# Two gated attention and expert layers on one core: the second normalisation moved to the next slot, and the work between the score products dealt out anew

## The chip, the cores and the metric

One core of one Trainium2 chip. The time is that of one execution on the device, in microseconds (us). Before the change three runs took 878.42, 873.18 and 877.70 us, median 877.7. The engines are TensorE (PE in the rows, its weight loads PEld), VectorE (DVE), ScalarE (ACT), GpSimd (POOL) and SyncE (SP), which issues most transfers.

## What is computed

32 sequences of 128 tokens, 128 wide, go through two layers. Cut to its core the reference is

```python
x = x + tanh(g_xattn[0]) * attention0(layernorm(x), ctx)   # 16 heads of 8, biases, output product Wo
x = x + tanh(g_ffn[0]) * experts0(layernorm(x))            # 8 experts, capacity routing, hidden 256
x = x + tanh(g_xattn[1]) * attention1(layernorm(x), ctx)   # 16 heads, no biases, no output product
x = x + tanh(g_ffn[1]) * experts1(layernorm(x))            # best 2 of 8 experts, hidden 512
```

The attentions are softmax(q k scale) v over 128 keys. The router of each expert layer is a product of the normalised tokens with a 128x8 matrix.

## The kernel before

Each layer has two stages: an attention stage over 16 pairs of sequences, and an expert stage over tiles of 256 tokens. The change touches only the attention stages.

**Slots.** An attention stage is a software pipeline. `pair_slots` walks 23 slots, p from -4 to 18, and in each slot every engine's `slot` function works on up to eight pairs, each at another step: n (four ahead) has its first normalisation's statistics taken, f (three ahead) is transposed and gets queries and keys, r (two ahead) its values' projection, m (one ahead) its score maxima, a (this one) the scores of its first sequence, b (one behind) those of its second sequence and the weighted values of both, z (two behind) its output and new x, and y (three behind) the router's product. A slot in which all are present is called full here: p from 3 to 11, and 12 but for n. The order on each engine is written out by hand and is a fixed queue; engines meet at semaphores (`wait_ge`).

**Units.** A slot has eight units. On TensorE unit i is `scores_for_maxima(i)` (L577: four products whose bank VectorE reduces, `maxima(i)`, L789), then a score product `scores` (L565: units 0 to 3 are the second sequence of b, numbers 4 to 7; units 4 to 7 the first of a), whose bank ScalarE turns into PT by an exponential (L443). There are two banks for each (MB, ST), so product i waits until number i-2 has been read. Between the units stand the fillers.

**Fillers of TensorE before.** Unit 0: the transpose of a's maxima MX, `values(b, 0)` (V0, L683, 16 products), the two transposes of OK (z, layer 0). Unit 1: the two transposes of XN (f). Unit 2: the output product (L613, z, layer 0, reads OKT) and the router's product (L619, y, reads NT, into bank PA). Unit 3: key and query products (L630, L632, f). Unit 4: V1. Unit 5: value projection (L647, r). Unit 6: four transposes of OT (b). Unit 7: the two transposes of N (z).

**ScalarE** copies between its exponentials: NT, OKT, XT (L461), LG (router's result, L466), HL (high halves of queries and keys, L474), OT (L484), VA (values, L490) and writes N, the second normalisation (L496, two instructions). **VectorE** between its maxima: MH (shifted maxima, L798), statistics of n (L774 to L806), the new x of z (L814), the statistics of z with MINUS and VE_N (L826, L827), the low halves of HL (L834), XN (L845) and the division by the sums of b (L854, L855, into OK). **GpSimd** raises the variances to the power -0.5 (L387, L391) and multiplies by minus the mean (L392); in layer 0 it adds the output bias to x (L398). **SyncE** sends MH into the row that the scores read (L298), loads the spread queries and keys (L306, L307) and writes HL out (L317). In layer 1 it also loads expert weights (L292) in eight slots.

PF is one bank for three uses: XN's transposes and the value projection in its first half, N's transposes in its second. Waits on `v_kept`, `front_kept` and `n_kept` keep its users apart.

## Time and profile before

| | us |
|---|---|
| median of three runs | 877.7 |
| lowest, highest | 873.18, 878.42 |
| the profiled execution's own time | 874.29 |
| its span in the profile | 872.5 |
| TensorE busy (matmul rows) | 536.8 (62%) |
| VectorE busy | 484.0 (55%) |
| ScalarE busy | 349.5 (40%) |
| GpSimd busy | 285.4 (33%) |

The span is 1.8 us shorter than the execution's time. The attention stages run from about 16 to 227 us and from about 400 to 595 us; in the expert stages and in the routing between them the change edits nothing. Busy shares over the whole span are means over stages that have different limits, so the rows further below are taken inside the attention stages.

### The profile page before, as it was taken

The page shows a single profiled execution, that of the slowest core. Times are in us where ns is not written, and L with a number is a line of the kernel's source. Part 1 is how long each engine was busy: PE and PEld are TensorE (multiplying, and loading weights), DVE is VectorE, ACT ScalarE, POOL GpSimd, SP SyncE. Part 2 cuts the span into 40 slices and gives each one's busy share as a digit, 9 for nine tenths or more (in the row PEclk, how much of TensorE's full clock was granted, in tenths as well). Part 3 has the DMA queues.
Part 4 walks back from the last instruction along what each step waited for, and adds up shares of the span by engine and source line. Part 5 has one row for each costly group of instructions (what it writes and reads, how often), then busy time and mean ns, then how long its engine had stood idle before and what let it go on. Part 6 is the DMA issues. An engine that isn't in the chain of part 4 may idle for free.

```text
span 872.5 us, 16776 instructions
## 1 busy us (share of the span) xinstructions
PE 536.8 (62%) x5459; PEld 427.9 (49%) x5459; DVE 484.0 (55%) x1521; ACT 349.5 (40%) x795; POOL 285.4 (33%) x342
## 2 busy tenths in 40 slices
PE   1688999987200008862798999861000199999960
PEld 0566666664100007651566667640000199999960
DVE  4668888874588203434789999847200034444324
ACT  1157777766100004321266777762000055555530
POOL 6102222201001754771011111010777435555550
PEclk9979999999555559995699999995555599999995
DMA  7543333320000312325455553200311212222219
GB/s 251 151 136 88 87 88 88 88 58 2 0 0 3 101 55 81 106 77 137 124 144 148 158 153 97 59 2 2 101 53 52 62 53 73 75 71 75 74 37 288
DMA packets 94628, 76.37 MB, mean 88 GB/s; under 512 B 13904, under 2 KB 88528, under 8 KB 94096
## 3 DMA queue, kind: packets, MB, share of 16 engines
q1 hardware_dynamic: 86432, 57.05, 24.0%
q0 software_dynamic: 7040, 14.53, 4.9%
q10 hardware_dynamic: 1072, 3.73, 1.3%
q8 instruction: 46, 0.75, 0.4%
q14 instruction: 38, 0.31, 0.1%
HBM read 45.54 MB, written 33.46 MB: 91 GB/s over the span
## 4 chain that ended last, share of the span: by engine, by line
PE 41%; POOL 15%; DVE 12%; issue 10%; DMA 9%; ACT 7%; SPq 4%; ACTq 1%; DVEq 0%; POOLq 0%
POOL dispatched L407 10%; PE bank L730 8%; PE bank L740 8%; PE bank L683 6%; PE bank L577 4%; PE bank L551 4%; POOL returned L414 4%; PE bank L565 4%; DMA QS_N<-MH 3%; DVE PT L979 2%; DVE MX L789 2%; ACT N L496 2%; DMA returned<-PT,META_ROW 2%; ACT PT L443 2%; PE bank L630 1%
## 5 line engine op out<-in xcount | busy, mean ns | idle before, releaser
L789 DVE TENSOR_REDUCE MX<-bank 128x4 f32<-128x512 f32 x256 | 172.9, 685 | 45.0 <-PE bank L577 44.8
L443 ACT ACTIVATE PT<-bank 128x512 f32<-128x512 f32 x256 | 152.7, 600 | 107.2 <-PE bank L565 106.4
L414 POOL DMA_INDIRECT returned<-PT,META_ROW x124 | 119.1, 961 | 111.8 <-DVE PT L1070 87.1
L521 ACT ACTIVATE XGT<-bank 128x256 f32<-128x256 f32 x62 | 23.8, 384 | 260.3 <-PE bank L551 260.3
L551 PE MATMUL bank<-CONST,PT 128*128 128x128 f32 x124 | 25.9, 292 | 148.2 <-issue 142.1
L577 PE MATMUL bank<-KS,QS_N 96*128 96x128 f16 x1024 | 104.8, 229 | 12.1 <-DMA KS<-spread 10.0
L565 PE MATMUL bank<-QS_N,KS 98*128 98x512 f16 x256 | 99.2, 391 | 8.2 <-DMA QS_N<-MH 7.8
L740 PEld LDWEIGHTS bank<-WALL,HT 128*128 128x128 f32 x808 | 98.8, 192 | 10.2 <-issue 7.0
L740 PE MATMUL bank<-WALL,HT 128*128 x808 | 101.1, 276 | 3.9 <-issue 1.5
L730 PE MATMUL bank<-XGT,XT_HL_WR 128*128 128x256 f32 x404 | 100.7, 389 | 0.0
L577 PEld LDWEIGHTS bank<-KS,QS_N 96*128 96x128 f16 x1024 | 78.5, 104 | 34.1 <-DMA KS<-spread 11.6
L1058 DVE COPY META_ROW<-PT 128x2 int32<-128x2 int32 x62 | 11.3, 182 | 150.8 <-DMA PT<-dispatched 111.4
L407 POOL DMA_INDIRECT dispatched<-N,SLOT x64 | 62.2, 971 | 96.7 <-DVE EX L1041 77.8
L551 PEld LDWEIGHTS bank<-CONST,PT 128*128 128x128 f32 x124 | 15.5, 149 | 152.9 <-issue 143.4
L730 PEld LDWEIGHTS bank<-XGT,XT_HL_WR 128*128 128x128 f32 x404 | 74.1, 196 | 7.9
L387 POOL TENSOR_TENSOR RSTD<-VE,EXPO 128x2 f32<-128x2 f32 x32 | 22.3, 698 | 156.0 <-DVE VE L806 155.9
L532 ACT ACTIVATE HT<-bank,XT_HL_WR 128x256 f32<-128x256 f32 x156 | 64.0, 472 | 21.4 <-PE bank L730 21.4
L683 PE MATMUL bank<-PT,VA 128*32 128x128 f32 x2048 | 69.6, 277 | 2.7 <-ACT LG L466 2.7
L391 POOL TENSOR_TENSOR RSTD_N<-VE_N,EXPO 128x2 f32<-128x2 f32 x32 | 22.1, 691 | 144.6 <-DVE VE_N L827 144.6
L683 PEld LDWEIGHTS bank<-PT,VA 128*32 128x32 f32 x2048 | 52.4, 110 | 20.3 <-issue 14.7
L1066 DVE TENSOR_TENSOR PT<-bank,WALL 128x256 f32<-128x256 f32 x39 | 16.6, 424 | 57.5 <-PE bank L740 52.5
L1053 DVE COPY XT_HL_WR<-WALL 128x516 f32 (+1 forms) x62 | 23.9, 385 | 31.2 <-issue 19.2
(172 smaller groups left out, 830.5 us busy)
## 6 DMA issues: line engine op xcount, KB each, us to landing
spread<-XT_HL_WR SPq DMA_DIRECT2D x128, 64.0 KB, 2.1
PT<-dispatched SPq DMA_DIRECT2D x62, 130.0 KB, 2.1
QS_N<-spread SPq DMA_DIRECT2D x128, 48.0 KB
KS<-spread SPq DMA_DIRECT2D x32, 192.0 KB
WALL<-in_w SPq DMA_DIRECT2D x8, 578.0 KB, 4.0
CT<-in_ctx SPq DMA_DIRECT2D x32, 128.0 KB, 2.7
spread<-XT_HL_WR SPq DMA_DIRECT2D x32, 128.0 KB, 2.3
dispatched<-in_pads SPq DMA_DIRECT2D x2, 1040.0 KB, 5.7
```

Source lines behind the costliest of these rows:

```text
L407: pool.indirect_dma_start(xs[layer][:, :], bass.IndirectOffsetOnAxis(ap=SLOT[:, k, b:b + 1], axis=0), (N, N2)[k][:, b, :], None).then_inc( ...
L414: pool.indirect_dma_start(ys[layer][:, :], bass.IndirectOffsetOnAxis(ap=META_ROW[:, a.f, c:c + 1], axis=0), YS[:, a.f, c, :], None).then_i ...
L443: nc.scalar.activation(PT[:, c, 4 * g:4 * g + 4, :].rearrange("p j q -> p (j q)"), ST[i % 2][:, :], ACT.Exp, scale=SCALE[layer]).then_inc( ...
L532: last = nc.scalar.activation(HT[:, a.u, m, :], bank[2 * a.u + m // 2][:, TILE * (m % 2):TILE * (m % 2) + TILE], ACT.Gelu, bias=WR[:, a.t, ...
L551: return nc.tensor.transpose(to, of, ident[0:n, 0:n])
L565: nc.tensor.matmul(ST[i % 2][:, :].rearrange("p (j q) -> p j q", j=J), KS[0:98, x.r, g, c * P:(c + 1) * P], QS[0:98, x.r, J * g:J * g + J, ...
L577: last = nc.tensor.matmul(MB[i % 2][:, j * P:(j + 1) * P], QS[0:96, m.r, J * g + j, c * P:(c + 1) * P], KS[0:96, m.r, g, c * P:(c + 1) * P ...
L683: last = nc.tensor.matmul(PA[32 * g:32 * g + 32, 256 * c + P * (j // 2):256 * c + P * (j // 2) + P], VA[:, b.r, c, head(g, j), :], PT[:, c ...
L730: last = nc.tensor.matmul(bank[2 * a.u + m // 2][:, TILE * (m % 2):TILE * (m % 2) + TILE], WR[:, a.t, m * P:(m + 1) * P], XGT[:, a.u, :], ...
L740: last = nc.tensor.matmul(bank[6 + a.u][:, c * D:(c + 1) * D], HT[:, a.u, m, c * P:(c + 1) * P], WALL[:, bass.ds(r + (W1COLS[layer] + m * ...
L789: V.tensor_reduce(out=MX[:, m.u, 2 * J * g + c:2 * J * (g + 1):2], in_=MB[i % 2][:, :].rearrange("p (j k) -> p j k", j=J), op=ALU.max, axi ...
L1053: V.tensor_copy(WR[:, a.t, 0:W1COLS[layer]], WALL[:, bass.ds(r, W1COLS[layer])]).then_inc(w_kept, 1)
```

## The change

It moves work between units and slots, and three small operations between engines:

- The second normalisation (N), its transposes and the router's product are now done in one slot, by pair y: N is written on ScalarE in unit 2, transposed in unit 4 ahead of that unit's score product, copied to NT after unit 5's exponential, and multiplied in unit 6. Before, N and its transposes came at the end of z's slot and the product in the next slot. The router's product now goes to bank PF instead of PA, and V1 has no wait for `lg_kept` any more.
- The division by the sums (reciprocal and OK) is done in slot z behind maxima 2, no longer in slot b behind maxima 7. OK's transposes are in unit 3, the output product in unit 5, the new x behind maxima 6, and its statistics behind maxima 7.
- TensorE's other fillers: XN's transposes to unit 0, V0 to unit 1, the value projection to unit 2, V1 to unit 5, OT's transposes to unit 7. Key and query products stay in unit 3. XN is made behind maxima 3, not 6.
- VE (one a slot), MINUS and VE_N (one each) are computed on GpSimd instead of VectorE. GpSimd's order within the slot becomes n, bias, z.

```diff
@@ GpSimd
                         pool.wait_ge(x_norm, before(n.g - 1))
+                        chain.link(nc.gpsimd.tensor_scalar(out=VE[:, n.u, :], in0=MV[:, n.u, :, 1], scalar1=LN_EPS, scalar2=None, op0=ALU.add))
                         nc.gpsimd.tensor_tensor(out=RSTD[:, n.u, :], in0=VE[:, n.u, :], in1=EXPO[:, :], op=ALU.pow).then_inc(x_rstd, 1)
...
+                    if z:
+                        pool.wait_ge(n_stats, z.g + 1)
+                        pool.wait_ge(n_copied, before(z.g - 1))
+                        nc.gpsimd.tensor_scalar(out=MINUS[:, z.u, :], in0=MV_N[:, z.u, :, 0], scalar1=-1.0, scalar2=None, op0=ALU.mult)
+                        chain.link(nc.gpsimd.tensor_scalar(out=VE_N[:, z.u, :], in0=MV_N[:, z.u, :, 1], scalar1=LN_EPS, scalar2=None, op0=ALU.add))
+                        chain.link(nc.gpsimd.tensor_tensor(out=RSTD_N[:, z.u, :], in0=VE_N[:, z.u, :], in1=EXPO[:, :], op=ALU.pow))
@@ ScalarE
+                    exponentials(b, 6)
+                    if y:
+                        act.wait_ge(n_rstd, y.g + 1)
+                        for c in range(2):
+                            last = nc.scalar.activation(N[:, y.b + c, 0:D], batch(y, c), ACT.Identity,
+                                                        scale=RSTD_N[:, y.u, c:c + 1], bias=OFFSET_N[:, y.u, c:c + 1])
+                        last.then_inc(n_copied, 1)
+
                     exponentials(b, 7)
...
@@ TensorE
                     scores_for_maxima(4)
+                    if y:
+                        pe.wait_ge(n_copied, y.g + 1)
+                        if r:
+                            pe.wait_ge(v_kept, r.g + 1)
+                        pe.wait_ge(lg_kept, y.g)
+                        for c in range(2):
+                            last = transpose(PF[:, 256 + c * P:256 + (c + 1) * P], N[:, y.b + c, 0:D])
+                        last.then_inc(n_t, 1)
                     scores(a, 0)
-                    if b:
-                        if y:
-                            pe.wait_ge(lg_kept, y.g + 1)
-                        values(b, 1)
...
+                    if y:
+                        pe.wait_ge(n_kept, y.g + 1)
+                        for c in range(2):
+                            last = nc.tensor.matmul(PF[:, 256 + E * c:256 + E * c + E], NT[:, c * P:(c + 1) * P],
+                                                    WG[:, layer, :], start=True, stop=True)
+                        last.then_inc(lg_done, 1)
@@ VectorE
-                        link(stats(n, STATS, MV[:, n.u]))
-                        V.tensor_scalar(out=VE[:, n.u, :], in0=MV[:, n.u, :, 1], scalar1=LN_EPS, scalar2=None,
-                                        op0=ALU.add).then_inc(x_stats, 1)
+                        stats(n, STATS, MV[:, n.u]).then_inc(x_stats, 1)
                     maxima(2)
+                    if z:
+                        dve.wait_ge(o_t, z.g + 1)
+                        dve.wait_ge(x_new, z.g)
+                        if layer == 0:
+                            dve.wait_ge(ok_t, z.g)
...
+                        stats(z, STATS_N, MV_N[:, z.u]).then_inc(n_stats, 1)
```

The removals mirror these additions. SyncE's queue is the same row for row. In the rows below "bank<-CONST,N" is a transpose of N, and the same for OK, OT, MX and XN; after the change the score products are L567, the products for maxima L579, transposes L553, and ScalarE's exponentials L446.

TensorE in layer 0, a full slot before, from the value projection of unit 5 to the end of unit 7:

```order
L647 MATMUL bank<-WSQ,CT 128x128 [waits v_kept,front_kept]
L647 MATMUL bank<-WSQ,CT 128x128
L577 MATMUL bank<-KS,QS_N 128x128 [waits m_read]
L577 MATMUL bank<-KS,QS_N 128x128 x3
L565 MATMUL bank<-QS_N,KS 128x512 [waits exp_done]
L551 MATMUL bank<-CONST,OT 128x128 [waits x_new,av_kept]
L551 MATMUL bank<-CONST,OT 128x128 x3
L577 MATMUL bank<-KS,QS_N 128x128 [waits m_read]
L577 MATMUL bank<-KS,QS_N 128x128 x3
L565 MATMUL bank<-QS_N,KS 128x512 [waits exp_done]
L551 MATMUL bank<-CONST,N 128x128 [waits front_kept,n_kept,v_kept,n_copied]
L551 MATMUL bank<-CONST,N 128x128
```

Each of the last two fillers follows, by one unit, the product that its copy waits for. The same engine after the change, from unit 3 to unit 4's scores:

```order
L579 MATMUL bank<-KS,QS_N 128x128 [waits m_read]
L579 MATMUL bank<-KS,QS_N 128x128 x3
L567 MATMUL bank<-QS_N,KS 128x512 [waits exp_done]
L624 MATMUL bank<-CT,WSQ 128x256 [waits m_split,hl_done,cx1]
L626 MATMUL bank<-XT_HL_WR,WSQ 128x256 [waits front_kept]
L553 MATMUL bank<-CONST,OK 128x128 [waits o_kept]
L553 MATMUL bank<-CONST,OK 128x128
L579 MATMUL bank<-KS,QS_N 128x128 [waits m_read]
L579 MATMUL bank<-KS,QS_N 128x128 x3
L553 MATMUL bank<-CONST,N 128x128 [waits lg_kept,v_kept,n_copied]
L553 MATMUL bank<-CONST,N 128x128
L567 MATMUL bank<-QS_N,KS 128x512 [waits exp_done,shift0]
```

N's transposes now stand ahead of a score product, and OK's ahead of unit 4. The rest of that slot, from unit 5 into unit 7:

```order
L579 MATMUL bank<-KS,QS_N 128x128 [waits m_read]
L579 MATMUL bank<-KS,QS_N 128x128 x3
L567 MATMUL bank<-QS_N,KS 128x512 [waits exp_done]
L683 MATMUL bank<-PT,VA 32x128 [waits exp_done]
L683 MATMUL bank<-PT,VA 32x128 x15
L651 MATMUL bank<-WSQ,OKT 128x128 [waits ok_kept]
L651 MATMUL bank<-WSQ,OKT 128x128
L579 MATMUL bank<-KS,QS_N 128x128 [waits m_read]
L579 MATMUL bank<-KS,QS_N 128x128 x3
L567 MATMUL bank<-QS_N,KS 128x512 [waits exp_done]
L660 MATMUL bank<-WG,NT 128x8 [waits n_kept]
L660 MATMUL bank<-WG,NT 128x8
```

The output product and the router's product, which stood next to each other, are now a unit apart, each behind another filler.

ScalarE in layer 0, before, from unit 3's exponential to N:

```order
L443 ACTIVATE PT<-bank 128x512 [waits s_banks]
L466 ACTIVATE LG<-bank 128x16 [waits lg_done]
L443 ACTIVATE PT<-bank 128x512 [waits av_done,s_banks]
L474 ACTIVATE XT_HL_WR<-bank,VEC 128x256 [waits written0,qk_done]
L474 ACTIVATE XT_HL_WR<-bank,VEC 128x256
L443 ACTIVATE PT<-bank 128x512 [waits s_banks]
L484 ACTIVATE OT<-bank 128x512 [waits o_t,av_done]
L443 ACTIVATE PT<-bank 128x512 [waits s_banks]
L490 ACTIVATE VA<-bank 128x16x2x8 [waits av_done,v_done]
L496 ACTIVATE N<-X,OFFSET_N,RSTD_N 128x128 [waits n_rstd]
L496 ACTIVATE N<-X,OFFSET_N,RSTD_N 128x128
```

And after, from unit 2's exponential:

```order
L446 ACTIVATE PT<-bank 128x512 [waits s_banks]
L460 ACTIVATE N<-X,OFFSET_N,RSTD_N 128x128 [waits n_rstd]
L460 ACTIVATE N<-X,OFFSET_N,RSTD_N 128x128
L446 ACTIVATE PT<-bank 128x512 [waits s_banks]
L468 ACTIVATE VA<-bank 128x16x2x8 [waits av_done,v_done]
L446 ACTIVATE PT<-bank 128x512 [waits av_done,s_banks]
L477 ACTIVATE XT_HL_WR<-bank,VEC 128x256 [waits written0,qk_done]
L477 ACTIVATE XT_HL_WR<-bank,VEC 128x256
L485 ACTIVATE OKT<-bank 128x256 [waits wo_done,ok_t]
L446 ACTIVATE PT<-bank 128x512 [waits s_banks]
```

N, which stood near the end of the slot behind the values' copy, now stands ahead of it and of unit 3's exponential; OKT has moved behind HL, and NT behind unit 5's exponential.

## Rows read from the trace of the kernel before

**Rows 1.** Busy time by stretch: full slots of layer 0, then of layer 1.

```profile
100.00:120.00 20.00, 17.99 (x250) 13.41 (x249) 17.80 (x55) 14.34 (x35) 3.94 (x7) 1.00 0.32 88
520.00:540.00 20.00, 18.58 (x263) 14.29 (x260) 19.13 (x61) 14.60 (x34) 3.16 (x6) 1.00 0.37 102
```

**Rows 2.** Timeline of ScalarE (start us, us): copies of OT, one a slot.

```profile
70.18 0.59 ACT L484 ACTIVATE OT<-bank 128x512 f32<-128x512 f32 x1
...
178.72 0.59 ACT L484 ACTIVATE OT<-bank 128x512 f32<-128x512 f32 x1
...
208.72 0.59 ACT L484 ACTIVATE OT<-bank 128x512 f32<-128x512 f32 x1
...
451.35 0.59 ACT L484 ACTIVATE OT<-bank 128x512 f32<-128x512 f32 x1
...
501.80 0.59 ACT L484 ACTIVATE OT<-bank 128x512 f32<-128x512 f32 x1
...
549.90 0.59 ACT L484 ACTIVATE OT<-bank 128x512 f32<-128x512 f32 x1
...
576.97 0.59 ACT L484 ACTIVATE OT<-bank 128x512 f32<-128x512 f32 x1
```

**Rows 3.** Waits, 70 to 178 us, then 446 to 550 (us, times, longest).

```profile
PEld bank L551 <- ACT N L496: 7.6, 10, 0.8
PEld bank L613 <- ACT OKT L456: 6.3, 10, 0.6
...
PEld bank L551 <- ACT OT L484: 6.2, 10, 0.6
...
PEld bank L565 <- DMA QS_N<-MH: 3.4, 5, 1.1
```

**Rows 4.** Timeline of TensorE in a full slot of layer 0.

```profile
104.91 0.44 PE L551 MATMUL bank<-CONST,N 128*128 128x128 f32 x2 [0.42 <-ACT N L496]
...
105.18 0.39 PE L577 MATMUL bank<-KS,QS_N 96*128 96x128 f16 x4
...
105.41 0.38 PE L565 MATMUL bank<-QS_N,KS 98*128 98x512 f16 x1
...
105.83 1.08 PE L683 MATMUL bank<-PT,VA 128*32 128x128 f32 x32
...
106.84 0.44 PE L551 MATMUL bank<-CONST,OK 128*128 128x128 f32 x2
...
108.68 0.71 PE L613 MATMUL bank<-WSQ,OKT 128*128 128x128 f32 x4 [0.30 <-ACT OKT L456]
...
109.23 0.51 PE L619 MATMUL bank<-WG,NT 128*128 128x8 f32 x4
...
109.60 0.38 PE L577 MATMUL bank<-KS,QS_N 96*128 96x128 f16 x4
...
110.90 0.39 PE L577 MATMUL bank<-KS,QS_N 96*128 96x128 f16 x4
```

**Rows 5.** Timeline of ScalarE in the same slot.

```profile
101.19 0.83 ACT L474 ACTIVATE XT_HL_WR<-bank,VEC 128x256 f16<-128x256 f32 x2
...
103.70 0.40 ACT L490 ACTIVATE VA<-bank 128x256 f32<-128x256 f32 x1
...
103.96 0.89 ACT L496 ACTIVATE N<-X,OFFSET_N,RSTD_N 128x128 f32<-128x128 f32 x2
...
105.83 0.60 ACT L443 ACTIVATE PT<-bank 128x512 f32<-128x512 f32 x1 [0.48 <-PE bank L565]
```

**Rows 6.** Groups by shape, GpSimd and VectorE (busy us, mean ns).

```profile
L391 POOL TENSOR_TENSOR RSTD_N<-VE_N,EXPO 128x2 f32<-128x2 f32 x32 | 22.1, 691 | 144.6 <-DVE VE_N L827 144.6
...
L377 POOL MEMSET QS_N<- 96x2048 f32 x4 | 7.3, 1825 | 0.2
...
L392 POOL TENSOR_TENSOR OFFSET_N<-MINUS,RSTD_N 128x2 f32<-128x2 f32 x32 | 6.3, 196 | 2.5
...
L806 DVE TENSOR_SCALAR VE<-MV 128x2 f32<-128x2 f32 x32 | 5.4, 169 | 1.1
```

More of the change, by code:

```diff
@@ L635, in slot @@
                     scores(a, 0)
[L636 to L639 removed]
                     scores_for_maxima(5)
                     scores(a, 1)
[L643 to L645 removed]
+                    if b:
+                        values(b, 1)
+                    if z and layer == 0:
+                        pe.wait_ge(ok_kept, z.g + 1)
@@ L653, in slot @@
+                    scores(a, 3)
                     if b:
@@ new lines, in slot @@
+                    maxima(3)
+                    if n:
+                        dve.wait_ge(x_rstd, n.g + 1)
+                        dve.wait_ge(front_t, before(n.g - 1))
+                        for c in range(2):
+                            last = V.tensor_scalar(out=XN[:, n.u, c * D:(c + 1) * D], in0=batch(n, c), scalar1=MV[:, n.u, c, 0:1],
+                                                   scalar2=RSTD[:, n.u, c:c + 1], op0=ALU.subtract, op1=ALU.mult)
+                        last.then_inc(x_norm, 1)
```

161 lines of the change are left out of this document (59 added, 102 removed).

## Prediction

> **What bounds the kernel now.** I began with the busy time by stretch [rows 1]. In full slots of the first attention stage TensorE's matmul rows are busy 18.0 of 20 us and VectorE 17.8, ScalarE 14.3; in the second stage it is 18.6, 19.1 and 14.6. The granted clock there is 1.00 of full speed, 2.4 GHz, so the clock is not what costs time here. Two engines stand near nine tenths, and neither is full: what is left is waits inside the slot.
>
> Second, the length of a slot, taken as the distance between two copies of OT (one a slot) [rows 2]. Layer 0: 70.18 to 178.72 is ten slots of 10.85 us; the three that follow, in which the fronts run out, take 30.0 together. Layer 1: 451.35 to 501.80 is five slots of 10.09, in which the expert weights are loaded beside the work; 501.80 to 549.90 five of 9.62; the next three take 27.1.
>
> Third, who TensorE waits for [rows 3]: three copies by ScalarE, once a slot each, 0.76, 0.63 and 0.62 us in the weight-load rows of ten slots: for N, for OKT (layer 0 alone) and for OT. Each copy is asked for one unit after the product that it copies, which is too soon. In time of the slot they are shorter, since part of it lies beside the product before. The timeline of a slot [rows 4] gives the price of the steps, from start to start: four products for the maxima 0.23, a score product and MX's transpose together 0.42 (I split it 0.22 and 0.20), a half of the values 1.01, N's pair of transposes 0.27, the output product 0.55, the router's 0.37. From 109.60 to 110.90 there is a unit's maxima and scores, 0.45, and so 0.85 for the key and query products. From these rows I estimate the rest: the value projection at half of the last, 0.43, the pairs for OK and XN like N's, OT's four transposes twice that, 0.54. Eight units of 0.445 and these (two halves of the values) sum to 9.37; the waits are 10.85 - 9.37 = 1.48, some 0.5 each.
>
> **The change, by the same rows.** TensorE loses and gains no instruction; V0 now follows a score product, as V1 did, which costs 0.09 more, so 9.46 without waits. What changes is how far each product stands behind its copy. I lay the new slot out from its first maxima product at 0. A score product is followed by its exponential 0.42 later (105.41, 105.83), ScalarE starts its next instruction 0.12 to 0.14 before the last one's end (103.70 + 0.40, 103.96), and TensorE goes on 0.05 after a copy's end [rows 4, 5].
> - N's transposes (unit 4). Unit 2's scores start at 2.69, the exponential at 3.11, the two N copies at 3.59 (0.89 for both), unit 3's exponential at 4.36, V's copy at 4.84, ending 5.24. TensorE, past the value projection (2.91), unit 3 (3.34), keys and queries (3.78), OK's transposes (4.63) and unit 4's maxima (4.90), comes to them at 5.13 and starts at 5.29: wait 0.16.
> - The output product (end of unit 5). Scores of unit 4 at 5.56, exponential 5.98, the two halves of HL at 6.46 (0.83), OKT at 7.17 (0.38, like V's copy), end 7.55. TensorE, after unit 5 and V1, is there at 7.32 and starts at 7.60: wait 0.28.
> - The router's product (unit 6) comes at 8.59, with NT's copy done at 8.29: no wait. Before, it stood right behind the output product and hid in its wait.
> - OT's transposes (unit 7). Unit 6's scores at 8.37, exponential 8.79, OT's copy 9.27 to 9.86. TensorE is there at 9.41: wait 0.50, as now.
> New layer 0 slot: 9.46 + 0.16 + 0.28 + 0.50 = 10.40, 0.45 less than 10.85. Ten slots give 4.5.
>
> VectorE: the three small operations on the variance and mean leave it, about 0.17 us each [rows 6], with two waits for its own results; it keeps 17.8/20 of 10.85 = 9.65 less about 0.4, so 9.2 in a slot: below 10.40. The division by the sums (reciprocal and OK) now stands behind maxima 2, done at about 4.3 (maxima 2 from 2.84, 0.6, two operations with 0.8), and its transposes are asked for at 4.6; X's update ends at about 9.65, before OT's transposes at 9.91. Both are covered, by some 0.3 us. If VectorE ran later than this, TensorE would wait for it here.
>
> Layer 1 has no OKT and no output product: 9.46 - 0.27 - 0.55 = 8.64, but with less in front of them N's pair waits 0.43, the router's product 0.07 and OT's 0.43: 9.57 against 9.62. The same sum for the kernel before (9.37 - 0.82 and two waits of 0.5) gives 9.55 where 9.62 was measured, so 0.07 is missing in it; five slots give between 0.25 and -0.1, and I take 0. In the slots beside the weight load, unit 4's scores wait for the two small transfers from MH (five times, up to 1.1 us [rows 3]). Between MX's transpose and that score TensorE does more than before: the value projection and N's pair with its wait, 1.1 us, come in, and the router's 0.37 goes behind. With 0.7 more cover most of the wait goes, and those slots come to the others' length: 5 x (10.09 - 9.62) = 2.4. If nothing of it goes, 0.
>
> SyncE's own order is the same. The spread reads are issued after MH's in both, and the sum above keeps hi and low parts of HL at 7.3 and 8.2 of the slot; I count nothing, and bound it at 0 to 0.3 us per layer 1 slot, should they land too late for a shorter slot.
>
> GpSimd: per slot it gets three operations of 128x2 more. The nearest row is the small product at 196 ns; the far one the fill of 96x2048 at 1825 ns [rows 6]. I take 0.2 each. VectorE's second statistics end 0.55 into the next slot; two such operations, the power of 0.69, the product of 0.20 and the gaps give the scale at 2.2, and ScalarE wants it at 3.59. So the cost is nothing, hidden beneath units 0 to 2, as long as one operation is under about 0.9. For the first normalisation the cover ends at 0.94.
>
> Fill and drain. Ahead of the ten slots of each layer stands one more that is nearly full; the two give 0.4 and 0.3. The drain slots, laid out in the same way, come to 9.9 + 9.4 + 8.3 = 27.6 for 30.0 and 25.8 for 27.1. That is 3.7 at most; these have less to hide behind, so the other end is 0, and I take 2.4. After the last pair the work is a chain with nothing beside it: GpSimd's operations on it cost two times 0.2 to 0.3 per layer, and N's pair stands ahead of the last output product: a loss of 0.5 per layer, 1.0 together. The first slots wait for transfers and XN; I count nothing, between -1 and +1.
>
> **Sum.** 4.5 + 0 + 2.4 + 0.7 + 2.4 - 1.0 = 9.0, against the profiled execution's 874.29: **865.3 us**. That execution is near the fast end of the runs shown, 3.4 under their median of 877.7; I keep its time as the base. About 1% (8.7 us) is what a measurement of this kernel can tell from no change.
>
> **Where the skill speaks against it.** The moved operations leave VectorE, but they run on GpSimd while VectorE works. In the rows of before the power on GpSimd has a mean of 691 ns beside a VectorE that is nine tenths busy [rows 1, 6]; whether VectorE is held while it runs, the rows do not tell. The Trainium skill (SBUF — State Buffer, Who interferes with whom) says that a VectorE instruction in a two-port mode, which `tensor_scalar` can be, and a GpSimd instruction shut each other out for their whole length, while VectorE's `tensor_reduce` never contends. By that rule the new operations are harmless where they fall beside maxima, which is where I expect all three; no run here shows them in their new places.
>
> **Rivals.**
> *The gain stays in layer 0 (870).* VectorE has 0.9 of 20 us idle in layer 1 [rows 1], 0.4 per slot. If the new operations on GpSimd hold VectorE back, 3 x 0.2 = 0.6 per slot, or if HL's second part now waits on ScalarE's first, layer 1 is bound as before; the drain gives nothing. What is left is 4.5 + 0.4 - 1.0 = 3.9, or 870.4; with 0.2 lost in each of ten slots of layer 1, 872. For it: VectorE's 19.1 of 20. Against: three operations leave it. That the change only moves its waits about, as my 0.50 for OT says of one of them, would end at 870 to 874 too. The skill's rule above is one way into this rival.
> *Slower, by GpSimd's chain (879).* N's copy now stands ahead of unit 3's exponential, V's copy and the first scores, so if the scale is late, everything is. It decides from 0.9 us per small operation. At 1.2 each the scale comes 0.6 late: 24 slots give 14 us, and with this in place of nothing 865.3 + 14 = 879; at the far row's 1.8, 1.9 late, 46 us, 910. For it: nothing stands between, and two engines feed it. Against: 196 ns in the nearest row.
> *More than forecast (859).* The waits of the three copies gone altogether in layer 0's ten slots would be 9.4 more; half of that, with all of the drain's 3.7, gives 859.
>
> **How the numbers follow.** The forecast with what lies around it, 861 to 869: 0.50. More: 0.10. Gain in layer 0 alone or moved waits: 0.29. Slower: 0.11. Faster by over 1% (under 865.6 by the execution's own time, under 869 by the median) takes all of the second, 0.40 of the first and 0.06 of the third: 0.56. Slower by over 1%: 0.10, the slower rival but for its mildest prices; within 1%: the rest, 0.34. The range 856 to 874 leaves out the slow rival and the ends of the others.
>
> **What would show it.** In the profile after: slots of the first layer at about 10.4; TensorE's wait for OKT halved, that for N near 0.3 in the weight-load rows, that for OT unchanged; no wait for POOL before N; layer 1 slots all near 9.6; VectorE's rows at L789 with more idle time ahead of them in layer 0. I am wrong if the slots stay above 10.6, if a wait for VectorE (OK, X, maxima) appears on TensorE, or if N waits for GpSimd.

## Result: 1.3% faster, and the profile after

The changed kernel took 863.02, 864.47, 866.71 and 866.29 us, median 865.38; the kernel before, with one more run on the same chip, has a median of 876.28. The ratio is 0.9869, with a 95% interval of 0.9841 to 0.9896 (the two medians alone differ by 10.9 us, or 1.2%). Two executions of the experiments below are not in their ratios, a slow one of e12 (910.81 us at a granted clock of 0.741, where the others have 0.825 to 0.830) and one of e9 that took 2696.48 us. The profiled execution took 863.02 us, its span is 861.2 where it was 872.5: 11.3 us less.

Busy time by stretch, in the columns of [rows 1]:

```profile
100.00:120.00 20.00, 18.91 (x261) 14.89 (x260) 17.82 (x50) 14.54 (x36) 6.02 (x14) 1.00 0.35 95
505.00:525.00 20.00, 19.11 (x284) 14.28 (x277) 18.96 (x51) 15.02 (x34) 5.19 (x14) 1.00 0.47 129
```

In the first layer TensorE went from 18.0 to 18.9 of 20 us busy, and VectorE stayed at 17.8: the same work in less time would have raised it to 18.7, but the three small operations are gone from it. In the second layer the row of 20 us shows 19.0 for VectorE, nearly as before, but that stretch is not a whole number of slots. Over five whole slots VectorE is busy 44.2 of 47.6 us (492.88 to 540.47), where it was 45.8 of 48.1 (501.80 to 549.90): it has a little more idle time there too.

Copies of OT on ScalarE, one a slot, as [rows 2]. The copy stands a unit later in its slot now, so only distances may be compared with before:

```profile
70.31 0.59 ACT L497 ACTIVATE OT<-bank 128x512 f32<-128x512 f32 x1
...
132.31 0.59 ACT L497 ACTIVATE OT<-bank 128x512 f32<-128x512 f32 x1
...
143.20 0.59 ACT L497 ACTIVATE OT<-bank 128x512 f32<-128x512 f32 x1
...
174.45 0.59 ACT L497 ACTIVATE OT<-bank 128x512 f32<-128x512 f32 x1
...
201.52 0.59 ACT L497 ACTIVATE OT<-bank 128x512 f32<-128x512 f32 x1
...
444.40 0.59 ACT L497 ACTIVATE OT<-bank 128x512 f32<-128x512 f32 x1
...
492.88 0.59 ACT L497 ACTIVATE OT<-bank 128x512 f32<-128x512 f32 x1
...
540.47 0.59 ACT L497 ACTIVATE OT<-bank 128x512 f32<-128x512 f32 x1
...
565.72 0.59 ACT L497 ACTIVATE OT<-bank 128x512 f32<-128x512 f32 x1
```

From 70.31 to 174.45 are ten slots, 104.1 us where there were 108.5. They are not alike: 70.31 to 132.31 is six of 10.33 each, and the one that follows takes 10.89. The three drain slots take 27.07 for 30.0. In layer 1 the five slots beside the weight loads take 48.5 for 50.5, the next five, called plain here, 47.6 for 48.1 (9.52 each), the three of the drain 25.25 for 27.1. (The eight loads are issued in slots 2 to 9, so the plain five have the last two of them beside them, in both kernels, and are hardly longer for it.)

Waits of TensorE's weight loads in layer 0, 70 to 170 us, to be held against [rows 3]:

```profile
PEld bank L553 <- ACT OT L497: 7.4, 10, 1.1
...
PEld bank L651 <- ACT OKT L485: 4.6, 9, 0.5
...
PEld bank L553 <- issue: 1.8, 9, 0.2
PEld bank L567 <- DMA QS_N<-MH: 0.8, 2, 0.6
```

The wait for N's two instructions is not in the list any more. What N's transposes still wait for stands under "issue", 0.2 in nine slots, and is read below. The wait for OKT has gone from 0.63 to 0.51 each, that for OT is longer (0.74 against 0.62 each). A new row stands at the end: scores that wait for MH's transfer, 0.8 us in two places of layer 0, one of which is the long slot.

The same slot of layer 0 as in [rows 4, 5], by its landmarks. It starts with its first maxima product at 102.44:

```profile
102.44 0.39 PE L579 MATMUL bank<-KS,QS_N 96*128 96x128 f16 x4
...
104.42 0.20 POOL L401 TENSOR_TENSOR OFFSET_N<-MINUS,RSTD_N 128x2 f32<-128x2 f32 x1
...
105.91 0.87 ACT L460 ACTIVATE N<-X,OFFSET_N,RSTD_N 128x128 f32<-128x128 f32 x2
...
107.16 0.38 ACT L468 ACTIVATE VA<-bank 128x256 f32<-128x256 f32 x1
...
107.61 0.20 PEld L553 LDWEIGHTS bank<-CONST,N 128*128 128x128 f32 x2 [0.20 <-issue]
107.64 0.41 PE L553 MATMUL bank<-CONST,N 128*128 128x128 f32 x2
...
109.95 0.71 PE L651 MATMUL bank<-WSQ,OKT 128*128 128x128 f32 x4 [0.24 <-ACT OKT L485]
...
110.95 0.51 PE L660 MATMUL bank<-WG,NT 128*128 128x8 f32 x4
...
111.64 0.59 ACT L497 ACTIVATE OT<-bank 128x512 f32<-128x512 f32 x1
```

N's scale is ready at 104.62, N begins at 105.91, its transposes at 107.64, the output product at 109.95, the router's at 110.95, OT's copy at 111.64. Counted from 102.44 these are 2.18, 3.47, 5.20, 7.51, 8.51 and 9.20.

N's transposes follow the end of V's copy (107.16 + 0.38 = 107.54) by 0.07 us, while N itself was written by 106.78; V's copy is one of the three things that they wait for (`v_kept`). In layer 1 it is the same with a longer wait: V's copy ends at 518.21, the weight load for N starts at 518.28 after 0.42 idle. The profile names no releaser in either place, but the times leave V's copy.

The operations that GpSimd took over (mean ns behind the busy time), as [rows 6]:

```profile
L398 POOL TENSOR_SCALAR MINUS<-MV_N 128x2 f32<-128x2 f32 x32 | 7.5, 233 | 182.2 <-DVE MV_N L777 182.2
...
L387 POOL TENSOR_SCALAR VE<-MV 128x2 f32<-128x2 f32 x32 | 7.0, 219 | 96.5 <-DVE MV L777 96.5
```

**Where 11.3 us came from,** by the same landmarks in both traces: ten full slots of layer 0 4.4; ten of layer 1 2.5 (2.0 of it beside the weight loads); the slot ahead of each ten 1.05; three drain slots of each layer 2.9 and 1.8; all else inside the attention stages 0.1; and between and behind the attention stages, where nothing was changed, 1.45 was lost.

Of the 1.05, some 0.7 is no gain of the change. The slot ahead of layer 0's ten took 10.60 before and 9.87 after, but in e9 below, whose layer 0 is the kernel before's, it took 9.94. In the kernel before the granted clock stood at 0.50, which is 1.2 GHz, from 58.0 to 61.5 us, and so within that slot (59.58 to 70.18); in e9 it was back at 1.00 by 61.0, where the slot begins (61.07).

### The profile page after: what moved, and what is told of

Its sections match the earlier page's. It is cut to its first block, busy times and chain, and to the rows that moved or that the text cites. A ratio compares the mean times of both kernels' runs of the same rounds, so it can differ in the third digit from the quotient of the medians.

```text
span 861.2 us, 16742 instructions
## 1 busy us (share of the span) xinstructions
PE 532.4 (62%) x5459; PEld 427.2 (50%) x5459; DVE 476.6 (55%) x1425; ACT 350.0 (41%) x795; POOL 308.3 (36%) x438
## 4 chain that ended last, share of the span: by engine, by line
PE 43%; POOL 15%; issue 10%; DVE 10%; DMA 10%; ACT 6%; SPq 5%; ACTq 1%; DVEq 0%; POOLq 0%
POOL dispatched L410 11%; PE bank L730 8%; PE bank L740 8%; PE bank L553 6%; PE bank L683 5%; PE bank L579 5%; PE bank L567 5%; POOL returned L417 4%; DMA QS_N<-MH 3%; DMA returned<-PT,META_ROW 2%; DVE PT L975 2%; ACT OT L497 2%; SPq L317 2%; PE bank L624 1%; PE bank L651 1%
## 5 line engine op out<-in xcount | busy, mean ns | idle before, releaser
L446 ACT ACTIVATE PT<-bank 128x512 f32<-128x512 f32 x256 | 151.7, 597 | 91.3 <-PE bank L567 90.1
L553 PE MATMUL bank<-CONST,PT 128*128 128x128 f32 x124 | 26.1, 294 | 147.7 <-issue 142.1
L579 PE MATMUL bank<-KS,QS_N 96*128 96x128 f16 x1024 | 103.1, 225 | 16.8 <-DMA KS<-spread 12.3
L567 PE MATMUL bank<-QS_N,KS 98*128 98x512 f16 x256 | 97.8, 387 | 6.4 <-DMA QS_N<-MH 6.1
L579 PEld LDWEIGHTS bank<-KS,QS_N 96*128 96x128 f16 x1024 | 76.8, 102 | 41.1 <-DMA KS<-spread 16.6
L553 PEld LDWEIGHTS bank<-CONST,PT 128*128 128x128 f32 x124 | 15.5, 148 | 152.2 <-issue 143.4
L398 POOL TENSOR_SCALAR MINUS<-MV_N 128x2 f32<-128x2 f32 x32 | 7.5, 233 | 182.2 <-DVE MV_N L777 182.2
L387 POOL TENSOR_SCALAR VE<-MV 128x2 f32<-128x2 f32 x32 | 7.0, 219 | 96.5 <-DVE MV L777 96.5
```

Of the source, the lines that this page charges most:

```text
L446: nc.scalar.activation(PT[:, c, 4 * g:4 * g + 4, :].rearrange("p j q -> p (j q)"), ST[i % 2][:, :], ACT.Exp, scale=SCALE[layer]).then_inc( ...
L553: return nc.tensor.transpose(to, of, ident[0:n, 0:n])
L567: nc.tensor.matmul(ST[i % 2][:, :].rearrange("p (j q) -> p j q", j=J), KS[0:98, x.r, g, c * P:(c + 1) * P], QS[0:98, x.r, J * g:J * g + J, ...
L579: last = nc.tensor.matmul(MB[i % 2][:, j * P:(j + 1) * P], QS[0:96, m.r, J * g + j, c * P:(c + 1) * P], KS[0:96, m.r, g, c * P:(c + 1) * P ...
```

## Experiments

Slot lengths are those of the profiled execution; ratios are to the kernel before on the same chip.

**e1: N's move alone.** To the kernel before; N's old block on ScalarE and the router's old product into PA go as well, and LG's copy moves to the end of the slot and reads PF:

```diff
                     exponentials(b, 4)
-                    if y:
-                        act.wait_ge(n_t, y.g + 1)
-                        act.wait_ge(lg_done, y.g)
-                        nc.scalar.activation(NT[:, :], PF[:, 256:512], ACT.Copy).then_inc(n_kept, 1)
...
+                    if y:
+                        act.wait_ge(n_rstd, y.g + 1)
+                        for c in range(2):
+                            last = nc.scalar.activation(N[:, y.b + c, 0:D], batch(y, c), ACT.Identity,
+                                                        scale=RSTD_N[:, y.u, c:c + 1], bias=OFFSET_N[:, y.u, c:c + 1])
+                        last.then_inc(n_copied, 1)
                     exponentials(b, 7)
...
                     exponentials(a, 0)
+                    if y:
+                        act.wait_ge(n_t, y.g + 1)
+                        act.wait_ge(lg_done, y.g)
+                        nc.scalar.activation(NT[:, :], PF[:, 256:512], ACT.Copy).then_inc(n_kept, 1)
...
                     scores_for_maxima(4)
+                    if y:
+                        pe.wait_ge(n_copied, y.g + 1)
...
+                            last = transpose(PF[:, 256 + c * P:256 + (c + 1) * P], N[:, y.b + c, 0:D])
+                        last.then_inc(n_t, 1)
                     scores(a, 0)
...
                     scores(a, 3)
-                    if z:
-                        pe.wait_ge(n_copied, z.g + 1)
+                    if y:
+                        pe.wait_ge(n_kept, y.g + 1)
...
-                            last = transpose(PF[:, 256 + c * P:256 + (c + 1) * P], N[:, z.b + c, 0:D])
-                        last.then_inc(n_t, 1)
+                            last = nc.tensor.matmul(PF[:, 256 + E * c:256 + E * c + E], NT[:, c * P:(c + 1) * P],
+                                                    WG[:, layer, :], start=True, stop=True)
+                        last.then_inc(lg_done, 1)
```

> The kernel before, with one part of the change alone: N, its transposes, NT and the router's product in y's slot (N behind the exponential of unit 2, transposes ahead of unit 4's scores, product at the slot's end into PF); every other filler stays. Theory (each wait of TensorE for a copy costs its length once a slot and is independent of the others): the wait for N, 0.5 to 0.6 us of the slot, goes, those for OKT and OT stay; layer 0 slots 10.85 to 10.3 or 10.4, layer 1 plain slots 9.62 to 9.1 or 9.2, in all 10 to 13 us faster than before, so as much as the whole change. Rival (the waits are one budget, and what one gives back the next takes, or VectorE does): slots fall by under 0.2 in layer 0 and not at all in layer 1, in all under 4 us.

Measured: 870.84 us, ratio 0.9949 (0.9921 to 0.9977), 5 us faster. In layer 0 the theory holds to the tenth: ten slots of 10.37, so one wait removed gives its 0.48, and the waits for OKT and OT stay as they were (0.63 and 0.62 each). That is practically all that the whole change gives in a full slot there, 0.52. In layer 1 the plain slots are 9.35 to 9.5, shorter than the changed kernel's own 9.5 (in e1 V's copy is not ahead of N's transposes, which start with no wait), but the slots beside the weight loads are 9.5 to 13.5. The total was forecast at twice what came or more. Its cause is in one row of the waits, 440 to 530 us, and in this piece of the timeline of its worst slot:

```profile
PE bank L564 <- DMA QS_N<-MH: 7.5, 6, 2.5
```

```profile
456.98 0.58 SPq L292 DMA_DIRECT2D WALL<-in_w  x1
457.76 1.20 SPq L298 DMA_DIRECT2D QS_N<-MH  x2
...
463.16 0.61 PE L564 MATMUL bank<-QS_N,KS 98*128 98x512 f16 x1 [2.49 <-DMA QS_N<-MH]
```

MH is sent out 0.8 us behind a weight load of 578 KB, and its scores begin 5.4 us later, 2.5 of it idle. The slot is 4.1 longer than a plain one, so the wait is not all of it: the granted clock was 1.00 until TensorE had stood idle in that wait, and 0.50 from about 462.5 to 469.5. (This execution, the profiled one, took 875.44 us, 4.6 over e1's median, so its stalls are above the usual.) The same place in the changed kernel:

```profile
494.72 0.59 SPq L292 DMA_DIRECT2D WALL<-in_w  x1
495.72 1.18 SPq L298 DMA_DIRECT2D QS_N<-MH  x2
```

```profile
499.45 0.38 PE L567 MATMUL bank<-QS_N,KS 98*128 98x512 f16 x1
```

There 3.7 us lie between issue and use and nothing waits. Without a stall it is 2.75 us in e1, 2.7 to 3.0 in the kernel before's plain slots, 3.7 in the changed one. So the moves of the other fillers, which give nothing in layer 0's full slots, are what covers this transfer in layer 1. e1 has less cover on one more ground: MH is sent 1.75 us behind its transpose, not 1.27, because VectorE still divides by the sums just before it takes up MH.

**e2: the three small operations back on VectorE,** in the changed kernel.

```diff
-                        nc.gpsimd.tensor_scalar(out=MINUS[:, z.u, :], in0=MV_N[:, z.u, :, 0], scalar1=-1.0, scalar2=None, op0=ALU.mult)
-                        chain.link(nc.gpsimd.tensor_scalar(out=VE_N[:, z.u, :], in0=MV_N[:, z.u, :, 1], scalar1=LN_EPS, scalar2=None, op0=ALU.add))
...
-                        stats(z, STATS_N, MV_N[:, z.u]).then_inc(n_stats, 1)
+                        link(stats(z, STATS_N, MV_N[:, z.u]))
+                        V.tensor_scalar(out=MINUS[:, z.u, :], in0=MV_N[:, z.u, :, 0], scalar1=-1.0, scalar2=None, op0=ALU.mult)
+                        V.tensor_scalar(out=VE_N[:, z.u, :], in0=MV_N[:, z.u, :, 1], scalar1=LN_EPS, scalar2=None,
+                                        op0=ALU.add).then_inc(n_stats, 1)
```

VE goes back in the same way.

> The changed kernel with its three small operations (VE, MINUS, VE_N) back on VectorE. Theory (VectorE is not what bounds the changed kernel): slots stay at 10.33 in layer 0, within 0.05, and at 9.5 in layer 1, within 0.1; the whole within 1.5 us of the changed kernel, that is 864 to 867. Rival (VectorE had become the bound and the move to GpSimd is where the gain is from): layer 1 slots back to 9.7 or more, the whole 3 to 8 us slower than the changed kernel, 868 to 873.

Measured: 862.31 us, ratio 0.9859 (0.9815 to 0.9904), within the interval of the changed kernel. Seven of its ten full slots of layer 0 are 10.33, three are 10.6 to 11.0, which are waits for MH. Of layer 1's plain slots two are 9.5, and three are 9.8 to 10.1 with waits for MH of 0.2 to 0.4 us: with the small operations back, VectorE sends MH 1.47 us behind its transpose, not 1.27. So one sign of the rival, slots of 9.7 or more, was there in part, but by a transfer and not by VectorE's share, and the total does not show it. The move to GpSimd is worth nothing in the total that can be measured. VectorE does not bound the changed kernel.

**e3: OT's copy before unit 6's exponential, not after it; e4: and X's update before maxima 6.** Both on the changed kernel:

```diff
-                    exponentials(a, 2)
                     if b:
                         act.wait_ge(av_done, 2 * b.g + 2)
                         act.wait_ge(o_t, b.g)
                         nc.scalar.activation(OT[:, :], PA[:, :], ACT.Copy).then_inc(av_kept, 1)
 
+                    exponentials(a, 2)
                     exponentials(a, 3)
```

And in e4 alone:

```diff
-                    maxima(6)
                     if z:
                         if layer == 0:
...
                                                    in1=two(z).rearrange("p c d -> p (c d)"), op0=ALU.mult, op1=ALU.add).then_inc(x_new, 1)
+                    maxima(6)
                     maxima(7)
```

> The changed kernel with OT's copy on ScalarE ahead of unit 6's exponential, not behind it. Theory (TensorE's last wait in each slot is for this copy alone, 0.37 us in time of the slot): in layer 1, where the new x waits for nothing of TensorE, slots go from 9.50 to 9.1 or 9.2; in layer 0 X's update, which ends 0.3 us before the transposes start, is next, and the slot goes from 10.33 to 10.1 or 10.25 with a wait for X on TensorE; in all 5 to 9 us faster than the changed kernel, 857 to 860. Rival (VectorE or the MH transfers bound the slot by now): no slot shorter by over 0.1, within 2 us of the changed kernel.

> As e3, and X's update on VectorE ahead of maxima 6 instead of behind it, so that it is done 0.6 us sooner. Theory: layer 0 slots at 9.95 to 10.05, no wait for X left; layer 1 as in e3; in all 2 to 4 us faster than e3. Rival (maxima 6, now later, holds the next maxima products; or MH's transfers are late): layer 0 no faster than e3.

Measured: e3 858.85 us, ratio 0.9827 (0.9786 to 0.9869). Layer 0 slots are 10.17, plain slots of layer 1 down to 9.15. TensorE's own rows in layer 0 name who is late next:

```profile
PE bank L553 <- DVE X L841: 2.8, 10, 0.6
PE bank L651 <- ACT OKT L485: 2.1, 9, 0.2
```

The transposes of OT now wait for X, 0.28 a slot, in the place that the theory gave. e4: 854.49, ratio 0.9775 (0.9731 to 0.9819), layer 0 slots 9.79. e4 is 4.4 us faster than e3, where 2 to 4 were expected, and no wait for X is left; its slot of layer 0 is shorter than the 9.95 that was expected. I had taken the wait from TensorE's rows, 0.37, which leave out what lies beside the product before. From start to start it is 0.53: in the changed kernel unit 7's score product starts at 111.53, takes 0.22 until the next can start, and OT's transposes start at 112.28. e4's slot is 0.54 shorter than 10.33. The plain theory, that each wait of TensorE for a copy is worth its length until the next in line is reached, is shown by both, with the length taken from start to start.

**e5 and e6: weight loads in slots 11 to 18** instead of 2 to 9, on e1 and on e4.

```diff
-                if 2 <= p < 2 + E:
-                    cols = slice((p - 2) * WCOLS[1], (p - 1) * WCOLS[1])
+                if 11 <= p < 11 + E:
+                    cols = slice((p - 11) * WCOLS[1], (p - 10) * WCOLS[1])
```

> e1 with the eight loads of layer 1's expert weights issued in slots 11 to 18 of its attention stage instead of slots 2 to 9, so that nearly all full slots run without them. Theory (in e1 layer 1's gain was eaten by late MH transfers, which queue behind the weight loads; TensorE's three waits are otherwise as in layer 0): slots 2 to 10 of layer 1 all at 9.3 to 9.4 us, MH waits under 1 us together where e1 had 7.5, and the whole 8 to 11 us faster than e1, 860 to 863. Rival (MH's transfers are late for another reason, or the loads when late delay the routing or the drain): slots still 9.6 or more, or the gain given back behind the attention stage, the whole within 3 us of e1.

> e4 with the same late weight loads. Theory: layer 1's full slots, 9.45 to 10.05 in e4, come to 9.1 or 9.2, ten slots of them, 4 to 6 us off e4's total: 848 to 851. Rival (layer 1 is at VectorE's bound near 9.5, or the late loads cost what they give): within 1.5 us of e4.

Measured: e5 872.05 us, ratio 0.9946 (0.9917 to 0.9974), which is e1's: the rival was right about the total. Of the nine slots that have no load now, five are 9.35, three 9.1 to 9.8 and one is 10.95 (it waits 1.4 for MH with no load near), but the loads took their stall with them: slots 11 to 14 take 12.07, 10.49, 12.11 and 12.10. The waits for MH in these four are 4.6 us together, about half of what they are too long; in and between them the granted clock stood at 0.50 three times, from 529 to 533, 549.5 to 557 and 563 to 567 us. e6: 853.41, ratio 0.9734 (0.9704 to 0.9763), 1 us off e4; five of the ten full slots are 9.15 or 9.16, the others up to 9.7, drain slots up to 10.9 (with the clock at 0.50 from 536.5 to 544). This is where my expectation failed in both: drain slots have no more cover for MH's transfer than full ones.

**e7 and e8: the power for RSTD_N done twice and four times,** in the changed kernel, to put the slower rival to the test; two executions each.

```diff
                         chain.link(nc.gpsimd.tensor_tensor(out=RSTD_N[:, z.u, :], in0=VE_N[:, z.u, :], in1=EXPO[:, :], op=ALU.pow))
+                        chain.link(nc.gpsimd.tensor_tensor(out=RSTD_N[:, z.u, :], in0=VE_N[:, z.u, :], in1=EXPO[:, :], op=ALU.pow))
                         nc.gpsimd.tensor_tensor(out=OFFSET_N[:, z.u, :], in0=MINUS[:, z.u, :], in1=RSTD_N[:, z.u, :],
```

This is e7; in e8 the added line stands three times.

> The changed kernel with the power for RSTD_N on GpSimd done twice in each slot (the same numbers written again), 0.8 us more ahead of N. Theory (in the profile after, the scale is ready 1.3 us before ScalarE takes it in a full slot): layer 0 slots stay at 10.33; the whole 0 to 2 us over the changed kernel, from the two ends. Rival (the slower rival of the prediction, a chain that has little cover): slots 0.3 to 0.8 longer.

> The same with the power done four times, 2.4 us more ahead of N. Theory: cover of 1.3 us is passed by 1.1, and N, the exponential of unit 3, V's copy, N's transposes and the scores of unit 4 all come later by that: layer 0 slots 11.3 to 11.5, the whole 20 to 30 us slower than the changed kernel, with a wait of ScalarE for OFFSET_N in each slot. Rival (ScalarE and TensorE make up for it within the slot): slots under 10.7.

Measured: e7 867.43 us, 2 over the changed kernel, ratio 0.9901 (0.987 to 0.9933), layer 0 slots 10.33 but for one of 10.8, and no wait of ScalarE for GpSimd in them. e8 909.41, ratio 1.0381 (1.0348 to 1.0413), slots of 11.37 in layer 0 and 10.55 in layer 1, with this row in ScalarE's waits of 70 to 170 us:

```profile
ACT N L463 <- POOL OFFSET_N L404: 8.4, 9, 0.9
```

The slots are as expected, each 1.04 longer. The total is not: 44 us over the changed kernel instead of 20 to 30. In the profiled execution, whose span is 46.7 longer, the twenty full slots take 19.1 of it; 17.9 are in the other slots up to the last copy of OT, above all in drain slots of up to 12.6, and 9.7 before the first copy and behind the last. Part of that is the clock, which stood at 0.50 from 193 to 197 and from 213.5 to 224 us, in the two longest slots of the drain. The mechanism of the slower rival is real, and its cover was 1.29 us in the trace (104.62 to 105.91).

**e9, e10 and e11: all eight weight loads behind the attention stage,** on the kernel before, on e1 and on e4.

```diff
-            pair_slots(1, attention_slot, matrices)
+            pair_slots(1, attention_slot)
+            for p in range(2, 2 + E):
+                matrices(p)
```

> The kernel before, with layer 1's eight weight loads issued by SyncE behind the whole attention stage instead of one a slot in slots 2 to 9. Theory (weight loads are what makes MH's transfers late in slots 2 to 7): ten full slots of layer 1 all at 9.6, so 5 x 0.47 = 2.4 us off before: 872 to 875, with nothing given back, since VectorE first needs the weights some 100 us after the stage. Rival (those slots are long for another reason, or routing is slowed by the loads): no gain, or a loss of 2 us or more.

> The same with e1's kernel. Theory (e1's steady slots are 9.35 in layer 1, and all that it lost against the changed kernel there is MH's transfers behind weight loads, for it has 2.75 us from MH's issue to its use where the changed kernel has 3.7): full slots 9.35, drain slots of e1 without their stalls, 7 to 11 us faster than e1: 860 to 864, equal to the changed kernel or better. Rival (e1's order is worse for other reasons as well, its drain or VectorE): 866 or more.

> The same with e4's kernel. Theory: full slots of layer 1 at 9.15 as in e6, without e6's long slots at the end of the stage: 5 to 7 us faster than e4, 848 to 850. Rival: within 2 us of e4 and e6, 852 to 855.

Measured: e9 871.63 us, ratio 0.996 (0.9944 to 0.9975). All ten full slots of layer 1 are 9.58: the 0.47 by which five of them were longer was the weight loads. The total gained 3.5, a little more than the 2.4 of these slots. e10: 865.38, ratio 0.9902 (0.9868 to 0.9935), 4 to 5 us faster than e1 and level with the changed kernel, just above the band that I gave. Two of its full slots are still 10.4 and 10.5 and a drain slot 11.4, with waits for MH of up to 1 us and no weight load near: with 2.75 us from issue to use the cover is short without them too. The drain slot is longer than its wait of 0.99 explains. These are the products of V1 behind its late score, and those of V0 in the next slot:

```profile
553.39 0.61 PE L566 MATMUL bank<-QS_N,KS 98*128 98x512 f16 x1 [0.99 <-DMA QS_N<-MH]
...
553.93 1.94 PE L684 MATMUL bank<-PT,VA 128*32 128x128 f32 x32
...
559.76 1.08 PE L684 MATMUL bank<-PT,VA 128*32 128x128 f32 x32
```

The same number of products takes 1.94 and then 1.08 us; the granted clock is 1.00 up to 553, 0.50 from there to 556.5, and 1.00 again. The stalls of 0.97 and 0.92 in e10's full slots left the clock at 1.00. So the theory had the larger part, not the whole.

e11: 849.17, ratio 0.9697 (0.9673 to 0.972), nearly all full slots 9.8 in layer 0 and 9.15 to 9.18 in layer 1 (the first there is 9.48); one drain slot of layer 0 is 10.7, with the clock at 0.50 from 175.5 to 179.5 us. It is the fastest of all, 3% under the kernel before and 16 us under the changed one:

```profile
100.00:120.00 20.00, 19.53 (x270) 15.58 (x270) 18.57 (x51) 15.81 (x37) 6.01 (x14) 1.00 0.36 100
505.00:525.00 20.00, 19.45 (x264) 15.08 (x263) 19.09 (x51) 15.66 (x36) 4.57 (x12) 1.00 0.36 97
```

TensorE is now at 19.5 of 20 in both layers. What is left of waits inside a full slot is OKT's 0.24 in layer 0; in layer 1 N's transposes still wait for V's copy (0.41 in the weight-load rows of e4, which has the same order) and the router's product 0.28 for NT's.

**e12: the router's product alone,** on the kernel before. The wait for LG's copy moves from V1 to the value projection and to N's transposes, which write PF next.

```diff
-                            last = nc.tensor.matmul(PA[:, 256 + E * c:256 + E * c + E], NT[:, c * P:(c + 1) * P],
-                                                    WG[:, layer, :], start=True, stop=True)
-                        last.then_inc(lg_done, 1)
 
                     scores_for_maxima(3)
                     scores(b, 7)
...
                         nc.tensor.matmul(PG[:, 0:256], WQ, XT[:, f.u, :], start=True, stop=True).then_inc(qk_done, 1)
+                    if y:
+                        pe.wait_ge(n_kept, y.g + 1)
+                        for c in range(2):
+                            last = nc.tensor.matmul(PF[:, 256 + E * c:256 + E * c + E], NT[:, c * P:(c + 1) * P],
+                                                    WG[:, layer, :], start=True, stop=True)
+                        last.then_inc(lg_done, 1)
 
                     scores_for_maxima(4)
                     scores(a, 0)
                     if b:
-                        if y:
-                            pe.wait_ge(lg_kept, y.g + 1)
                         values(b, 1)
```

> The kernel before, with the router's product alone changed: it goes to bank PF behind the key and query products of unit 3, and V1 no longer waits for its result to be copied out of PA. Theory (in full slots V1 never waited for it; in the last slots of each stage it did, for 0.5 to 0.8 us each, and that is part of what the drain gained over the forecast): full slots 10.85 and 9.62 within 0.05, the drain (slots 13 to 16) 1 to 3 us shorter in both layers together. Rival (the drain's gain has another source): drain slots unchanged, under 0.5 us in all.

Measured: 876.17 us, ratio 1.0004 (0.9975 to 1.0033). In layer 0 the full slots stay at 10.85 and the four of the drain lose 0.4 each, 1.7 together. In the kernel before those waits are one row (TensorE, 180 to 225 us):

```profile
PE bank L683 <- ACT LG L466: 1.9, 4, 0.8
```

In layer 1 the expectation failed: plain slots went from 9.62 to 9.93, and the three drain slots did not get shorter (27.25 for 27.1). The router's product had stood between XN's transposes and the query product and had given ScalarE time to copy XT. Without it TensorE waits (weight loads, 490 to 550 us):

```profile
PEld bank L626 <- ACT XT_HL_WR L461: 2.5, 6, 0.4
```

## Why the prediction was right, point by point

865.3 us were forecast and 865.38 measured. The mechanism was right, but an agreement within 0.1 us is luck: the forecast took 9.0 off the profiled execution's 874.29, and the medians fell by 10.9, from 876.28. The gain was forecast some 2 us too small and from a base 2 us too low, and the two errors cancel. Between the profiled executions the gain was 11.3, and the terms below are of these two.

- **The slot of layer 0, 10.40 forecast.** Measured 10.33, in a slot whose landmarks fell within 0.12 of the layout: N 3.59 (3.47), N's transposes 5.29 (5.20), output product 7.60 (7.51), router 8.59 (8.51), OT's copy 9.27 (9.20). The offset comes from steps that I had to estimate: MX's transpose takes 0.11 for the 0.20 of my split, XN's pair 0.22 for 0.27; the value projection was near (0.45 for 0.43). The waits, from start to start: N's transposes 0.16 forecast, 0.22 found, and for V's copy, as laid out; OKT 0.28, found 0.30; router none, none; OT 0.50, found 0.53. The steps without waits were thus some 0.2 shorter than the 9.46 of the forecast (whose 9.37 is 9.33 if each unit is put at the stated 0.445). The ten slots gave 4.4 for 4.5, but by another way: ten slots of 10.33 would have given 5.2, and only seven are 10.33; one of 10.89 and two of over 10.4 took 0.8 back. e1 shows that N's wait was the whole of this term.
- **"I count nothing" for MH's transfer in layer 0** was a miss. Between MX's transpose and the score that reads MH the output product with its wait and the router's product went out (1.2 us in all), the value projection and N's pair came in (0.7); so the cover there went from 5.5 us to 5.0, and in this profile the three slots over 10.33 pay 0.8 together; e2 has three such slots too.
- **Layer 1 plain slots, 0 forecast, 0.5 measured** (9.52 for 9.62). A small miss within the bounds named; e3 and e1 show that VectorE was not the limit at 9.5, since slots of 9.15 and 9.35 are had with the same work on it or more. N's transposes wait 0.43 there from start to start, as forecast.
- **The slot ahead of each ten, 0.7 forecast, 1.05 measured.** As said, some 0.7 of this is where the low clock fell in the kernel before, so the change shows no more than 0.4 of it.
- **Slots beside the weight loads, 2.4 forecast, 2.0 measured.** The mechanism is shown by e9 (no loads, no long slots) and e1 (less cover, longer slots; there with the clock's share). The cover grew by 1.0 from issue to use, where I had reckoned 0.7.
- **Drain, 2.4 forecast, 4.75 measured.** This is the term that was mis-sized. I laid the slots out and had 3.7, took a part, and missed what comes on top: V1 no longer waits for the router's result to be copied. e12 puts 1.3 of it on that in layer 0's three slots (0.4 each), and nothing in layer 1's.
- **Serial ends, -1.0 forecast, about +0.1 measured.** The last pair's chain in layer 0 is longer, as forecast (9.7 to 12.3 us from its OT copy to its router result), but slot 16 before it gave back 2.2, part of it again V1's wait.
- **GpSimd, hidden.** Right: 219 to 233 ns each for the 200 assumed, cover 1.29 for 1.4; e7 stays inside it, e8 passes it and each full slot costs what a late scale costs.
- **The signs named.** No wait for GpSimd before N in full slots, and OT's wait about as it was, came true. TensorE's wait for OKT was to be halved and went from 0.63 to 0.51. VectorE's maxima were to have more idle time ahead of them in layer 0 and have less: 6.1 us between 70 and 170 us, where it was 9.5, for VectorE's work and the slot shrank together. A wait for VectorE, which was to mean that I am wrong, is in no full slot, but two drain slots of layer 0 wait for OK (1.2 us together).
- **What was not in the sum:** 1.45 us lost outside the attention stages. No edit reaches there, and single executions of one kernel differ by 3 us and more, so its cause stays open.

Of the rivals, "the gain stays in layer 0" is refuted for the changed kernel (6.0 of 11.3 came in layer 1's stage), and its cause, VectorE held by GpSimd, by e2: without GpSimd's new operations the total is the same within the intervals. In the slot above MINUS and VE_N (from 103.04 to 103.55) fall beside a maximum (102.94, 0.69 us), and VE (105.49) beside the one at 105.32 (0.66). The maxima of layer 0's full slots take 680 ns on average, where they took 686, GpSimd's powers 708, where they took 692 and 702. The Trainium skill's rule on the shared port (SBUF — State Buffer, Who interferes with whom), by which `tensor_reduce` never contends with GpSimd, agrees with these rows. The slower rival needs operations of 0.9 us and they take 0.22.

Open: how much of e10's remaining stalls is the spread transfers and how much SyncE's queue, and why e1's executions scatter by 8 us. That a stall is sometimes followed by some 4 to 7 us at half clock, as in the profiled executions of e1, e5, e6 and e10, is a candidate for the scatter; only one execution of each has a profile, so it is not shown.

## What to carry to other kernels

In a software pipeline with fixed queues, lay one slot out by start-to-start times and ask for each filler how long its operand has been ready: a product moved further from its copy, or a copy moved ahead by one exponential, gave its wait, 0.5 us a slot (e1, e4), while moving 0.17 us operations off a busy engine gave nothing that the total shows. Take a wait from start to start, for the idle time in the rows leaves part of it out. Count the distance from each transfer's issue to its use as well, for a reorder that shortens it loses in some slots what it wins in all. When a slot is longer than its waits explain, look at the granted clock of that stretch. And look at fill and drain slots apart: there a wait that full slots hide stands open, and a copy that another filler hid by chance (e12) shows itself only when that filler is moved.

## Not expected

- The pair of small transfers for MH (8 KB each) took 2.7 us from issue to use where nothing waited and up to 5.4 behind a 578 KB load issued 0.8 us before it on the same queue; and up to 4.3 with no such load near (the long slot of layer 0 in the changed kernel, and e5's slot of 10.95).
- Moving the weight loads by nine slots moved their stall of 1 to 2.7 us a slot with them; only behind the stage, where no small transfer is urgent, did they cost nothing that showed.
- After a stall of TensorE for MH the granted clock in some cases fell from 1.00 to 0.50, that is from 2.4 to 1.2 GHz: after 2.49 us idle in e1, 1.60, 1.55 and 1.03 in e5, 0.99 in e10. After others it did not (2.08, 1.30 and 1.12 in e1, 0.97 and 0.92 in e10). While it is down a half of the values takes 1.94 us instead of 1.08, so such a stall costs more than its length.
